# The convolution kernel's high and low halves as pairs in one tile, read by TensorE with a step of two

## The reference

```python
# stage 1: one of 16 matrices per sequence
W = weights[condition]                                # (B, 128, 128)
x = x + einsum('bct,bcd->bdt', x, W)

# stage 2: a long convolution per channel, masked by the sequence's length
mask = arange(2048) < length[:, None]
u_m = x * mask
kernel = _get_kernel(log_dt, C, log_A_real, A_imag, 2048)   # (H, 2048): 2*Re(sum_n Cs * exp(dtA * t))
y = irfft(rfft(u_m, 4096) * rfft(kernel, 4096))[..., :2048] + u_m * D[:, None]
x = x + y * mask
```

## Time and profile before

| | us |
|---|---|
| median of 3 runs | 2311.28 |
| lowest and highest of them | 2309.85 and 2313.21 |
| the profiled execution's own time | 2319.77 |
| its span, first to last instruction | 2318.0 |
| TensorE busy | 2173.3 (94%) |
| TensorE's weight loads busy (beside the matmuls) | 1881.8 (81%) |
| VectorE busy | 1643.2 (71%) |
| ScalarE busy | 1472.1 (64%) |
| GpSimd busy | 1177.7 (51%) |

### The profile page before, as it was taken

One profiled execution on the slowest core, in us unless ns is written; L12 is line 12 of the kernel. 1 busy time (PEld: TensorE's weight loads), 2 busy tenths in 40 slices (PEclk: granted clock), 3 DMA queues, 4 the chain that ended last, 5 costly groups with the idle time before them and its releaser, 6 DMA issues.

```text
span 2318.0 us, 62100 instructions
## 1 busy us (share of the span) xinstructions
PE 2173.3 (94%) x15101; PEld 1881.8 (81%) x15101; DVE 1643.2 (71%) x3359; ACT 1472.1 (64%) x4354; POOL 1177.7 (51%) x1862
## 2 busy tenths in 40 slices
PE   6777777999999999999999999999999999999999
PEld 2222225888888888888888888899999999999999
DVE  4999303777777777777777777667777777777776
ACT  4555546777777777777777777545555555555555
POOL 0994502666666666666666666423333333333332
PEclk9999999999999999999999999999999999999999
DMA  8999999999999999999999999889999999999997
GB/s 326 419 393 363 410 356 333 319 316 320 317 320 322 321 320 320 322 319 324 323 323 321 316 321 320 255 250 269 275 277 269 272 277 272 267 266 274 275 269 231
DMA packets 355876, 716.27 MB, mean 309 GB/s; under 512 B 41602, under 2 KB 172932, under 8 KB 355844
## 3 DMA queue, kind: packets, MB, share of 16 engines
q1 hardware_dynamic: 300548, 514.55, 72.9%
q10 hardware_dynamic: 55296, 201.35, 21.5%
HBM read 395.92 MB, written 319.82 MB: 309 GB/s over the span
## 4 chain that ended last, share of the span: by engine, by line
PE 58%; DMA 15%; SPq 6%; issue 5%; DVE 5%; ACT 5%; ACTq 5%; DVEq 0%
PE bank L909 12%; PE bank L910 11%; PE bank L911 11%; DMA toep<-k_scratch 8%; PE bank L954 7%; PE bank L946 6%; PE bank L891 5%; PE bank L878 5%; DMA row_x<-in_x 3%; DVE decay L812 2%; ACTq L524 2%; DMA decay<-x_scratch 2%; SPq L339 2%; DMA out<-decay 1%; SPq L356 1%
## 5 line engine op out<-in xcount | busy, mean ns | idle before, releaser
L800 DVE TENSOR_TENSOR u_lo<-bank,u_hi 128x512 fp32r<-128x512 f32 x512 | 351.9, 687 | 209.6 <-ACT u_hi L606 206.2
L954 PE MATMUL bank<-toep,u_odd 128*128 128x128 f32 x2048 | 392.7, 273 | 0.0
L812 DVE COPY_PREDICATED decay<-mask,bank 128x512 f32<-128x512 uint8 x512 | 378.2, 739 | 11.2 <-PE bank L911 3.8
L909 PE MATMUL bank<-t_hi,u_hi 128*128 128x256 f32 x1024 | 360.6, 352 | 23.9 <-DMA toep<-k_scratch 23.2
L549 ACT ACTIVATE row_y<-bank 128x512 f32<-128x512 f32 x512 | 301.4, 589 | 124.0 <-ACT row_y L549 56.6
L492 POOL TENSOR_TENSOR x_lo<-row_x,x_hi 128x256 fp32r<-128x256 f32 x496 | 371.7, 780 | 0.0
L878 PE MATMUL bank<-row_x,w_sel 128*128 128x512 f32 x528 | 267.2, 635 | 94.0 <-ACT w_sel L525 49.0
L806 DVE TENSOR_TENSOR s_lo<-state,s_hi 128x128 fp32r<-128x128 f32 x768 | 238.2, 310 | 159.9 <-ACT s_hi L618 157.2
L469 POOL TENSOR_TENSOR outer<-par 128x256 f32<-128x256 f32 x512 | 315.5, 637 | 20.5
L466 POOL COPY par<-table 128x71 f32 (+1 forms) x256 | 61.9, 242 | 510.1 <-PE bank L911 510.1
L954 PEld LDWEIGHTS bank<-toep,u_odd 128*128 128x128 f32 x2048 | 313.7, 189 | 0.0
(11 more groups left out here) (139 smaller groups left out, 5376.3 us busy)
## 6 DMA issues: line engine op xcount, KB each, us to landing
row_x<-in_x SPq DMA_DIRECT2D x256, 512.0 KB, 6.0
x_scratch<-row_y ACTq DMA_DIRECT2D x256, 512.0 KB, 5.6
decay<-x_scratch SPq DMA_DIRECT2D x256, 512.0 KB, 5.9
out<-decay SPq DMA_DIRECT2D x256, 256.0 KB, 4.4
out<-decay ACTq DMA_DIRECT2D x128, 512.0 KB, 5.6
b_scratch<-b_mat SPq DMA_DIRECT2D x128, 256.0 KB, 6.1
t_hi<-k_scratch SPq DMA_DIRECT2D x256, 128.0 KB, 4.8
t_lo<-k_scratch SPq DMA_DIRECT2D x256, 128.0 KB, 4.5
```

What stands on the lines that cost most here:

```text
L800: v.tensor_tensor(u_lo[j % 2][:, blocks, :], t_bank[q][:, :].rearrange("s (k b) -> s k b", b=B), u_hi[j % 2][:, blocks, :].bitcast(fp32), ...
L812: v.copy_predicated(tile[j][:, cols], mask[:, seg * SEG + q * BANK:seg * SEG + (q + 1) * BANK], y_bank[q][:, :]).then_inc(y_taken, 1)
L909: mm(to, w_hi, m_hi, start=start, stop=False, skip_group_check=True)
L954: mm(y[:, P:CHUNK], u_odd[i][:, c, :], toep[j][:, P - 1::-1], start=False, stop=True, skip_group_check=True)
```

## The change

The taps' high and low halves are written side by side, as 384 pairs (high, low), behind the run of whole numbers. Their zero padding is set by a memset of its own. `t_hi` and `t_lo` are replaced by one tile `t_pair` of 128 x 256 x 2, loaded by one DMA of 512 numbers a partition (skewed by two numbers a partition). TensorE reads element 0 or 1 of each pair, still backwards. The semaphore counts 32 in place of 48 a channel. `halve_k` and `split_k` write, and `split_k` also reads, with a step of two. Layout of `k_dram`, number of bytes and order of all other work are as before.

```diff
-        k_rows = [sb(f"k_rows{i}", [COPIES, 3, KROW]) for i in range(2)]
+        k_rows = [sb(f"k_rows{i}", [COPIES, 3 * KROW]) for i in range(2)]
+        k_whole = [r[:, 0:KROW] for r in k_rows]
+        k_pairs = [r[:, KROW:3 * KROW].rearrange("s (w n) -> s w n", n=2) for r in k_rows]
         toep = [sb(f"toep{i}", [P, P]) for i in range(SLOTS)]
-        t_hi = [sb(f"t_hi{i}", [P, CHUNK], fp32r) for i in range(SLOTS)]
-        t_lo = [sb(f"t_lo{i}", [P, CHUNK], fp32r) for i in range(SLOTS)]
+        t_pair = [sb(f"t_pair{i}", [P, CHUNK, 2], fp32r) for i in range(SLOTS)]
...
                 row = k_dram[bass.ds(k - seg * H, 1), 0:1, 0:1]
-                for n, dst, first in ((1, t_hi[j][:, :].bitcast(fp32), 0), (2, t_lo[j][:, :].bitcast(fp32), 0), (0, toep[j][:, :], P)):
-                    skewed = bass.AP(row.tensor, row.offset + (n * KROW + first), [[3 * KROW + P // COPIES, COPIES], [1, P // COPIES], [1, CHUNK - first]])
+                pairs = t_pair[j][:, :, :].bitcast(fp32).rearrange("s w n -> s (w n)")
+                for dst, at, step, width in ((pairs, KROW, 2, 2 * CHUNK), (toep[j][:, :], P, 1, P)):
+                    skewed = bass.AP(row.tensor, row.offset + at, [[3 * KROW + step * P // COPIES, COPIES], [step, P // COPIES], [1, width]])
                     sp.dma_start(dst, skewed).then_inc(toep_loaded[j], 16)
...
-                pool.memset(k_rows[i][:, :, CHUNK:KROW], 0.0).then_inc(pads_zeroed, 1)
+                pool.memset(k_whole[i][:, CHUNK:KROW], 0.0)
+                pool.memset(k_pairs[i][:, CHUNK:KROW, :], 0.0).then_inc(pads_zeroed, 1)
...
-                v.tensor_copy(row[:, 1, 0:CHUNK].bitcast(fp32r), row[:, 0, 0:CHUNK]).then_inc(k_half, 1)
+                v.tensor_copy(pairs[:, 0:CHUNK, 0].bitcast(fp32r), whole[:, 0:CHUNK]).then_inc(k_half, 1)
...
-                v.tensor_tensor(row[:, 2, 0:CHUNK].bitcast(fp32r), row[:, 0, 0:CHUNK], row[:, 1, 0:CHUNK], ALU.subtract).then_inc(k_ready, 1)
+                v.tensor_tensor(pairs[:, 0:CHUNK, 1].bitcast(fp32r), whole[:, 0:CHUNK], pairs[:, 0:CHUNK, 0], ALU.subtract).then_inc(k_ready, 1)
...
-                split_mm(y, u_hi[i][:, 2 * c, :], u_lo[i][:, 2 * c, :], t_hi[j][:, CHUNK - 1::-1], t_lo[j][:, CHUNK - 1::-1], start=(c % 2 == 0), stop=False)
+                split_mm(y, u_hi[i][:, 2 * c, :], u_lo[i][:, 2 * c, :], t_pair[j][:, CHUNK - 1::-1, 0], t_pair[j][:, CHUNK - 1::-1, 1], start=(c % 2 == 0), stop=False)
...
-                    pe.wait_ge(toep_loaded[j], k * 12 + (48 - j * 12))
+                    pe.wait_ge(toep_loaded[j], k * 8 + (32 - j * 8))
```

More of the change, by code:

```diff
@@ L328, in store_kernel @@
                 sp.wait_ge(k_ready, k + 1)
-                sp.dma_start(k_dram[bass.ds(k, 1), :, :].rearrange("a s w -> (a s) w"), k_rows[i][:, :, :].rearrange("s n w -> s (n w)")).then_inc(k_stored[i], 16)
+                sp.dma_start(k_dram[bass.ds(k, 1), :, :].rearrange("a s w -> (a s) w"), k_rows[i][:, :]).then_inc(k_stored[i], 16)
             def load_toeplitz(seg, k, j, gd):
@@ L775, in keep_k @@
                     dve.wait_ge(k_stored[i], k * 8 - i * 8)
-                v.scalar_tensor_tensor(k_rows[i][:, 0, 0:CHUNK], delta[0:COPIES, CHUNK - 1::-1], par[j][0:COPIES, COL_DP:COL_DP + 1],
+                v.scalar_tensor_tensor(k_whole[i][:, 0:CHUNK], delta[0:COPIES, CHUNK - 1::-1], par[j][0:COPIES, COL_DP:COL_DP + 1],
                                        k_part[0:COPIES, :], ALU.mult, ALU.add).then_inc(k_made, 1)
             def halve_k(k, j):
-                row = k_rows[j % 2]
+                whole, pairs = k_whole[j % 2], k_pairs[j % 2]
                 dve.wait_ge(k_made, k + 1)
-                v.tensor_copy(row[:, 1, 0:CHUNK].bitcast(fp32r), row[:, 0, 0:CHUNK]).then_inc(k_half, 1)
+                v.tensor_copy(pairs[:, 0:CHUNK, 0].bitcast(fp32r), whole[:, 0:CHUNK]).then_inc(k_half, 1)
             def split_k(k, j):
-                row = k_rows[j % 2]
+                whole, pairs = k_whole[j % 2], k_pairs[j % 2]
                 dve.wait_ge(k_half, k + 1)
-                v.tensor_tensor(row[:, 2, 0:CHUNK].bitcast(fp32r), row[:, 0, 0:CHUNK], row[:, 1, 0:CHUNK], ALU.subtract).then_inc(k_ready, 1)
+                v.tensor_tensor(pairs[:, 0:CHUNK, 1].bitcast(fp32r), whole[:, 0:CHUNK], pairs[:, 0:CHUNK, 0], ALU.subtract).then_inc(k_ready, 1)
             def split_b(k, j):
```

## The result

The changed kernel takes **2586.38 us** (median of 4 runs, 2584.29 to 2590.74), the kernel before, beside it on the same chip, 2310.57 us (2309.62 to 2313.21). The ratio is 1.1194 with an interval from 1.1175 to 1.1214: 276 us slower, where 23 us faster was forecast. The time of the first rival, 2614 us, is the one that lies near. Two runs further on (6625.35 us in f1, 2933.29 us in the kernel before beside it) took far longer than all others of their kernels and are left out of the ratios.

What follows compares the result with a forecast made beforehand. TensorE was taken as the bound, interrupted in the first half by waits for toep. An earlier toep gave 23 us, all other terms 0: from 2311.28 us to 2288 us, range 2267 to 2313 us, leaving out a dear read.

Steps and rivals of the forecast that it cites:

- the first rival: TensorE reads pairs at half rate, 0.11 us more a matmul in both halves: about 2614 us; half rate or dearer read: 0.20.
- TensorE reads with a step of minus two: 3,072 matmuls on the pairs read every second number backwards: taken as 0, far bound 0.11 us more a matmul.
- threshold of 7.5 ns: Extra time for each of the 3,072 matmuls on pairs beyond which the forecast gain is lost.
- The 23 us from an earlier toep: First half: toep issued 0.73 us earlier, 0.5 us of it reaching TensorE, gaining 23 us.
- a landing of over 5.3 us: Sign in the changed kernel's profile: toep's landing rising from 4.8 to over 5.3 us means the bytes decided.
- the second rival: toep lands after the bytes ahead, however early issued: 2311 us; chance 0.09, shared with VectorE's longer copy undoing the gain.
- The loss in the stretch: TensorE's time lost to waits for toep, 600 to 1400 us: 24.6 us, 0.27 us a channel.
- the waits for VectorE's taking of y: TensorE's waits in the first half, 7.5 us, ranked next after those for toep, far behind.
- two thirds of the 35 us: Share of the first half's 35 us lost to toep that a shift by 0.5 us would gain: 23 us.
- VectorE's strided writes: Halving and splitting write with a step of two: taken as 0, upper bound for the copy 0.13 us a channel.
- The memsets: Two more memsets by GpSimd at the start, said to vanish in its long waits.
- fewer descriptors: Pair load with 128 descriptors of 2 KB in place of 256 of 1 KB, counted in favour of a shorter landing.

Runs made afterwards that it cites:

- f1: Kernel before, with t_hi, the pad and t_lo loaded as one piece by one DMA, one issue less and 64 KB more a channel: 2328.81 us, ratio 1.0069.
- w2: Kernel before, but the matmuls on t_hi and t_lo read a constant tile of zeros backwards with a step of two: 2577.74 us.
- x_lines: Kernel before, those matmuls reading zeros forwards: 2 of 4 numbers, 4 of 8 begun 8 bytes off a 16-byte border, 6 of 8: 2496.73 us.
- e1: Changed kernel, but TensorE reads two unbroken runs of 256 numbers of the pair tile backwards with a step of one: 2308.49 us, ratio 0.9999.
- e3: Kernel before, with only the high half of b stored and loaded, 128 KB less a channel, all issues in place: 2303.19 us, ratio 0.9977.
- f2: Kernel before, with all three Toeplitz tiles loaded by one DMA, 448 KB in place of 320 KB: 2359.28 us, ratio 1.0227.
- wp: Kernel before, those matmuls reading zeros backwards as aligned pairs, two of every four numbers: 2586.84 us.
- e2: Changed kernel, strided read kept, but the pairs loaded in two halves, so three Toeplitz issues a channel: 2586.10 us, ratio 1.1187.
- f5: Kernel before, with the store of b issued behind the store of k_rows on SyncE's queue, no byte changed: ratio 1.0062.

## Why the prediction was wrong, step by step

**TensorE reads with a step of minus two: the step that failed.** It was taken at 0 with 0.11 us a matmul as its far bound. The measured surplus is 0.32 us for three matmuls, 0.107 us each, so the far bound was the truth, and w2 shows it without the rest of the change. The wrong turn was the row that the choice leaned on: a strided read by VectorE was taken as the nearest row for a read by TensorE. VectorE spends 224 to 226 ns on 64 elements there, where TensorE takes 256 columns in 120 ns: at that pace a read at half rate needn't be seen, and another engine's read says little of TensorE's. The sentence that nothing but distance changes (4 bytes to 8, "still short") was no argument either, since a distance of 32 bytes costs no more than 8. The Trainium skill's rule ("SBUF — State Buffer", section "Door 1: The DMA port swizzle"), two hits in a line of 16 bytes for full rate, called the read free. The lines of 16 bytes are there, as x_lines shows by moving one pattern by 8 bytes, but for TensorE's moving operand two hits give 0.23 us a matmul and four give 0.12 us. The measurement decides.

**The first rival's working** held: in the second half 169 us were forecast and 165 measured; in the first half 134 and 106. There the longer matmuls swallowed more slack than the 0.27 us a channel that was counted. They add 1.30 us a channel (in the second half channels begin 7.55 us apart in place of 6.25 us), and by the table 0.22 us of waits for toep and 0.20 us of waits for states vanish in the first half: 1.30 - 0.42 = 0.88 us, which is 9.70 - 8.82. Its chance of 0.20 was too low for an operation that 3,072 matmuls on the bound engine depend on and that no row showed; by the prediction's own threshold of 7.5 ns, only a price of almost exactly nothing kept the sign.

**The 23 us from an earlier toep were wrong too**, which the loss hid and e1 uncovered. The issue moved up as stated (1.98 us after b's store instead of 2.76; in the median 1.79 instead of 2.65). The step that failed is the landing, where 0.5 of the 0.73 us were to reach TensorE because "most of the 4 to 5 us of landing is no transfer time". One transfer alone would be 0.2 to 0.4 us, but toep lands behind what stands ahead of it on the queue, and those bytes stayed: from b's issue to toep's landing it is 7.4 us before and 7.5 us in e1, 7.9 us with 64 KB more (f1) and 7.0 us with 128 KB less (e3). The prediction named the sign to look for, a landing of over 5.3 us; e1 shows 5.8. That is the second rival, "the queue of bytes decides": e1 at a ratio of 0.9999 is its 2311 us. The loss in the stretch was sized about right (24.6 us; by the starts of the matmuls it is 0.22 x 91 = 20 us). The issue saved became an idle queue: the wait of SyncE's queue for k_rows grew from 57.8 us to 135.8 us in e1, by 0.86 us a channel.

**A wait was overlooked.** The prediction has the waits for VectorE's taking of y (7.5 us) come next after toep's, "far behind". In the same view the wait for ScalarE's state, 21.1 us in 55 places, stands between them; neither nor the sum has it. It costs 0.20 us a channel, nearly as much as toep, and it grows when toep's shrinks (e3). There the waits for toep fell by 14.7 us in the stretch, and the whole kernel gained 5 us. So the next step, from a shift of 0.5 us to two thirds of the 35 us, had no ground either.

**VectorE's strided writes** were right at 0: 278 ns for 274, and 406 for 403. The memsets left no sign (the first copy begins 6 us earlier than before), and fewer descriptors brought nothing that e1 would show.

## What to carry to other kernels

Before the moving operand of a matmul is laid out anew, count how many of its numbers TensorE takes from each aligned 16 bytes: interleaving two 4-byte tiles halved the rate here, while aligned runs of four would have kept it, so a tile can be shared by blocks of four numbers but not number by number. And where the DMA engines' share is near 1 and the GB/s don't change from one version to the next, ask of a late transfer what bytes stand ahead of it on its queue: here moving its issue up by 0.86 us only lengthened its landing. A full share alone proves no bound (in f2's second half it is 1.01, and TensorE is busy for all 500 of the 500 us from 1700 to 2200 us). Before a wait is priced, list every other wait of that engine in the same view: here the next one took its place.

## What the runs showed that was not expected

- The moving read has two rates with the edge between two and four numbers a line: 256 columns in 0.12 us with four, 0.23 to 0.25 us with two or one. Direction doesn't matter: two of four numbers backwards (wp) and forwards (the first matmul of x_lines) both begin 0.28 us ahead of the next, where a read in one piece begins 0.21 us ahead.
- A step of 8 numbers was a little cheaper than one of 4, 0.22 against 0.24 us a matmul and 2530 against 2604 us in all, one run each. I have no explanation.
- VectorE wrote every second 4-byte number at the price of writing all (278 against 274 ns for 16x256).
- toep's 64 KB take anything from 2.8 to 6.1 us to land, counted from its own issue: 4.4 us at a share of 0.95 (e3), 5.4 at 0.94 in the changed kernel, 4.8 at 0.97 before, 5.8 at 0.99 (e1), 6.1 at 1.00 (f1), 5.3 at 1.00 (f5). Neither its size nor the mean share tells which. An issue that moves up while the work ahead of it stays makes this number larger with no byte later: counted from b's issue, the changed kernel has 6.9 us with one Toeplitz load ahead of toep and e2 6.7 us with two, though its own landing is 5.4 us in the one and 4.4 us in the other.
